# A source-block pass on one core: q rows of 3 of 13 cell groups gathered by GpSimd instead of multiplied by TensorE

## The chip, the cores and the metric

One core of a Trainium2 chip runs the whole program. The metric is the time of one execution in microseconds; three runs of the kernel before took 3949.36 to 3950.79 us, median 3950.47. Differences of the change are small, so all times are given to 0.1 us.

## The reference

The program is two graph layers with a layer norm behind each. The change touches the first:

```python
row, col = edge_index                       # 200,000 edges, 6,250 nodes, sorted by col
ef = concat([x[row], x[col], edge_attr])    # 128 + 128 + 2 features
h = ef @ W1 + b1                            # = p[row] + q[col] + attr @ W1[256:]
h = relu((h - mean(h)) * rsqrt(var(h) + 1e-5) * gamma + beta)
msgs = h @ W2 + b2
out = segment_sum(msgs, row) / (count(row) + 1) + x
```

p and q are x times the two halves of W1, so an edge's hidden row is a sum of a row of p (by its source), a row of q (by its target) and a product of its two attributes. The second layer is three graph convolutions, which the change leaves alone.

## The kernel before, in words

The 6,250 nodes make 49 blocks of 128. The bucket pass (`drive` with `step`, about 100 to 1250 us) sorts the edges into cells: a cell (source block b, target block c) has 128 slots, and for every slot it writes the place of its source and of its target within the block, and the attributes, to DRAM (`lrow_dram`, `arow_dram`). In each of its steps ScalarE copies TensorE's result `pbk` to `lo_all` (L997) and to `cells` (L998), and TensorE's next product (L873) waits for the latter.

The source-block pass (phase two, 1303 to 2655 us) goes over the 49 source blocks b, and in a block over 13 groups of cells: 12 of four cells, the last of one. Four quarters of T (`QUARTERS`: groups 0-2, 3-5, 6-8, 9-12) hold the places of source (T[k][:, 0]) and target (T[k][:, 1]) of every slot, spread over the partitions by a broadcast DMA from SP (L1237); VectorE turns them into 0/1 matrices by one compare (L1427).

For a group g each engine does, in its own order written out by hand:
- TensorE, `hidden(g)`: the attributes' product into a PSUM bank (L1291), then for each cell three matmuls with p (L1296) and three with q (L1298), since p and q are held as three bf16 parts each. Then `sums(g - 3)`: each cell's z times `hotf`, the 0/1 matrix of slots to sources, into `pSum` (L1312).
- ScalarE: Relu of the bank, rounded to bf16 (L1347, semaphore z_hi); then `middle(g - 1)`, which rounds what is left over (L1340, z_mid).
- VectorE: `left(g)` (L1439), bank minus z_hi, to `res` (z_res); then `low(g - 1)` (L1444), `res` minus z_mid, the third part of z (z_low). After g = 3 comes `quarter(b, 3)`, after g = 4 `take_sum` (L1450, L1452), after g = 6, 9, 12 `quarter(b + 1, 0..2)`; a quarter is the compare of T (L1427) and that of `hotf` (L1434).
- GpSimd does nothing in this pass; in the bucket pass it adds an identity to one 128x128 tile a step (L779).

There are four full PSUM banks (and `z`, `res` buffers), group g using number g % 4, and one small one for group 12. `sums(g)` waits for z_low of g, and TensorE may take the bank of g - 4 once `left` has read it.

Of the kernel before, what the change touches and what calls it, by code (L numbers as in the profile page):

```python
# [19 lines left out]
F32 = mybir.dt.float32  # L20
# [9 lines left out]
ROWS = B * P  # L30
# [21 lines left out]
QCELLS = (12, 12, 12, 13)  # L52
STRIP = 512
# [474 lines left out]
def build(nc, t, out):  # L528
# [7 lines left out]
    with outer:  # L536
        def mk(ctx):
# [36 lines left out]
             chunk_used y_taken yt_ready tail_done ln_ask ln_root out_ready out_sent dv3 root_b x_in bias_done g_taken""".split()})  # L574
        t_in = [fit_sem(f"t_in{u}") for u in range(4)]
        attr_rows = [fit_sem(f"attr_rows{u}") for u in range(2)]
        a_in = [fit_sem(f"a_in{u}") for u in range(7)]
# [32 lines left out]
        with early:  # L610
            sb, _ = mk(early)
            q3 = sb("q3", [P, B, 3, D], BF16)
            q3_flat = q3[:].rearrange("p b m d -> p (b m d)")
            prod_raw = sb("prod_raw", [P, 2 * 4 * TPB * B], BF16)
# [16 lines left out]
            with one:  # L631
# [17 lines left out]
                class Carve:  # L649
# [3 lines left out]
                    def take(self, n):  # L653
# [31 lines left out]
                q3st = [sb(f"q3st{u}", [P, 4, 3, D], BF16) for u in range(2)] + [q3_flat[:, NF * COLS:NF * COLS + 12 * D].rearrange("p (b m d) -> p b m d", b=4, m=3)]  # L685
                q3st.append(in_x1f.take(6 * D).bitcast(BF16).rearrange("p (b m d) -> p b m d", b=4, m=3))
                q3_sent = q3_out + [S["pf_in"]]
# [12 lines left out]
                          (pid1[:], t["pid1"])]  # L700
# [7 lines left out]
                def sp_1(sp):  # L708
# [64 lines left out]
                def pool_1(pool):  # L773
# [7 lines left out]
                    drive(pool, step)  # L781

# [121 lines left out]
                def act_1(act):  # L904
# [52 lines left out]
                    def step(s, m, par, bkt, h_, a_, y_, st_):  # L957
# [33 lines left out]
                        if bkt:  # L991
# [5 lines left out]
                            nc.scalar.activation(lo_all[:, :, s:s + 1] if isinstance(s, int) else lo_all[:, :, bass.ds(s, 1)], got[:, 0:1, :].rearrange("p f b -> p b f"), ACT.Copy)  # L997
                            nc.scalar.activation(cells[par][:, 0:8, 0:B], got, ACT.Copy).then_inc(S["cells_ready"], 1)  # L998
                    drive(act, step)
# [185 lines left out]
            with two:  # L1185
# [17 lines left out]
                st = ps("st", [P, 512])  # L1203

# [20 lines left out]
                def sp_2(sp):  # L1225
# [8 lines left out]
                    def quarter(b, k):  # L1234
                        c0 = 4 * QUARTERS[k][0]
                        rows = lrow_dram[b:b + 1] if isinstance(b, int) else lrow_dram[bass.ds(b, 1)]
                        sp.dma_start(T[k], rows[:, :, c0:c0 + QCELLS[k], :].rearrange("a f c s -> a f (c s)").to_broadcast([P, 2, QCELLS[k] * P])).then_inc(t_in[k], 16)  # L1237
# [19 lines left out]

                def pe_2(pe):
# [17 lines left out]
                    pe.wait_ge(S["q3_in"], 16)  # L1276
# [594 lines left out]
```

## Time and profile before

| | us |
|---|---|
| median of 3 runs | 3950.47 |
| profiled execution | 3951.36 |
| its span, first to last instruction | 3949.5 |
| TensorE (PE) busy over the span | 3769.3 |
| VectorE (DVE) busy | 2573.1 |
| ScalarE (ACT) busy | 1395.4 |
| GpSimd (POOL) busy | 85.1 |

Busy times are sums of durations of single instructions, seen as one where they overlap. Matmuls are pipelined: each of 128 columns is shown as 220 ns long, while a new one starts every 55 ns. So the pace of TensorE is read from the chain of waits, whose pieces don't overlap. L numbers are lines of the kernel before.

### The profile page before, as it was taken

To read this page: it belongs to the slowest core of one execution; us is meant where nothing else is said; L and a number is where in the kernel's file an instruction comes from. 1 tells how busy PE (TensorE), PEld (TensorE's weight loads), DVE (VectorE), ACT (ScalarE), POOL (GpSimd) and SP (SyncE) were. 2 spreads that over 40 slices of the span, in tenths; PEclk is the share of its full clock that TensorE was granted. 3 is DMA by queue.
4 is the path that set the end of the run, shared out by engine and by line. 5 is a ranking of instruction groups with operands and counts; after the bars stand their busy time and mean duration, and the time that the engine had idled before them with its cause. 6 is when DMAs were issued, how large, how long until landed. Compare 5 with 4: busy or idle time off the path is not lost.

```text
span 3949.5 us, 104146 instructions
## 1 busy us (share of the span) xinstructions
PE 3769.3 (95%) x42510; PEld 2695.9 (68%) x42510; DVE 2573.1 (65%) x3609; ACT 1395.4 (35%) x3527; POOL 85.1 (2%) x53
## 2 busy tenths in 40 slices
PE   4699999999998799999999999997999999999999
PEld 3488888888887688887888888884444444454444
DVE  7999999999993688888888888875111111111222
ACT  5355555545543355554555455545000000000000
POOL 0000000000000000000000000000000000000000
PEclk9899999999998899999999999999999999999999
DMA  7123223232233733333333333334666566656664
GB/s 238 51 83 99 84 87 93 84 96 88 81 98 140 122 126 129 133 122 125 124 132 131 124 126 129 126 114 144 196 196 197 188 199 196 196 189 207 211 204 139
DMA packets 397700, 547.34 MB, mean 139 GB/s; under 512 B 175743, under 2 KB 335240, under 8 KB 390440
## 3 DMA queue, kind: packets, MB, share of 16 engines
q1 hardware_dynamic: 390856, 537.51, 42.9%
q10 hardware_dynamic: 6624, 6.42, 0.5%
q8 instruction: 196, 3.21, 0.3%
q14 instruction: 24, 0.20, 0.0%
HBM read 434.34 MB, written 109.53 MB: 138 GB/s over the span
## 4 chain that ended last, share of the span: by engine, by line
PE 91%; DVE 4%; SPq 2%; ACT 1%; issue 1%; DMA 1%; ACTq 0%; DVEq 0%
PE py L1579 29%; PE pY L835 10%; PE ph L1298 10%; PE ph L1296 10%; PE pSum L1312 10%; PE pbk L896 8%; PE pA L822 3%; PE ph L1291 3%; PE pX L827 2%; PE pS L826 1%; PE pbk L873 1%; PE ptr L881 1%; DVE prod_raw L1120 1%; PE pg L1567 1%; SPq L1245 1%
## 5 line engine op out<-in xcount | busy, mean ns | idle before, releaser
L1579 PE MATMUL py<-ring_raw,p 128*128 128x512 bf16 (+1 forms) x3822 | 783.4, 367 | 18.0 <-DVE dummy L1739 16.1
L1298 PE MATMUL ph<-q,prod_raw 128*128 128x128 bf16 x7056 | 781.7, 220 | 0.8 <-issue 0.8
L1296 PE MATMUL ph<-p,prod_raw 128*128 (+1 forms) x7056 | 780.9, 220 | 0.0
L1579 PEld LDWEIGHTS py<-ring_raw,p 128*128 128x128 bf16 x3822 | 362.2, 98 | 430.9 <-DVE dummy L1739 16.5
L1296 PEld LDWEIGHTS ph<-p,prod_raw 128*128 128x128 bf16 x7056 | 518.6, 98 | 110.9 <-issue 2.7
L1347 ACT ACTIVATE x<-ph 128x512 bf16<-128x512 f32 x588 | 351.2, 597 | 668.0 <-PE ph L1298 664.7
L1439 DVE SCALAR_TENSOR_TENSOR ring_raw<-ph,x 128x512 f32<-128x512 f32 x588 | 404.3, 688 | 182.0 <-ACT x L1347 170.8
L1312 PE MATMUL pSum<-x,ring_raw 128*128 128x384 bf16 x2401 | 499.6, 327 | 8.9 <-DVE x L1444 8.9
L835 PE MATMUL pY<-p,ring_raw 128*128 128x128 bf16 x7203 | 501.0, 219 | 0.2 <-issue 0.2
L1298 PEld LDWEIGHTS ph<-q,prod_raw 128*128 128x128 bf16 x7056 | 495.8, 98 | 0.0
L1755 DVE TENSOR_TENSOR yt<-py,dinv_row 128x512 f32<-128x512 f32 (+1 forms) x39 | 25.8, 661 | 697.1 <-PE py L1579 697.1
L955 ACT ACTIVATE ring_raw<-pA 128x512 bf16<-128x512 f32 (+1 forms) x637 | 357.9, 571 | 250.5 <-PE pA L822 247.7
L1444 DVE TENSOR_TENSOR x<-ring_raw,x 128x512 bf16<-128x512 f32 (+1 forms) x637 | 414.4, 651 | 0.1
L835 PEld LDWEIGHTS pY<-p,ring_raw 128*128 128x128 bf16 x7203 | 409.3, 97 | 0.4 <-issue 0.4
L1579 PE MATMUL py<-ring_raw,g 128*128 128x512 bf16 (+1 forms) x1911 | 392.8, 368 | 1.9 <-DVE dummy L1767 1.9
L1632 ACT ACTIVATE hT<-yt,cb 128x512 f32<-128x512 f32 (+1 forms) x39 | 27.2, 697 | 1036.9 <-DVE yt L1755 1036.9
L1340 ACT ACTIVATE x<-ring_raw 128x512 bf16<-128x512 f32 (+1 forms) x637 | 381.4, 599 | 11.9 <-DVE ring_raw L1439 10.4
L1120 DVE TENSOR_TENSOR prod_raw<-q 128x1666 bf16<-128x1666 bf16 x392 | 375.5, 1020 | 12.7 <-PE pbk L896 11.6
L1093 DVE TENSOR_TENSOR ring_raw<-iota_lo,x 128x3584 bf16<-128x3584 bf16 x196 | 355.1, 1872 | 12.7 <-PE pX L827 12.7
L896 PE MATMUL pbk<-prod_raw,q 128*128 128x392 bf16 x1666 | 321.7, 350 | 28.1 <-DVE q L1093 28.1
L1579 PEld LDWEIGHTS py<-ring_raw,g 128*128 128x128 bf16 x1911 | 181.4, 98 | 209.0 <-issue 2.2
L896 PEld LDWEIGHTS pbk<-prod_raw,q 128*128 128x128 bf16 x1666 | 161.5, 98 | 170.2 <-issue 35.6
(322 smaller groups left out, 3906.0 us busy)
## 6 DMA issues: line engine op xcount, KB each, us to landing
ring_raw<-at_dram SPq DMA_DIRECT2D x252, 896.0 KB, 4.8
prod_raw<-lrow_dram SPq DMA_DIRECT2D x147, 768.0 KB, 4.2
at_dram<-ring_raw SPq DMA_DIRECT2D x49, 1568.0 KB, 5.6
prod_raw<-lrow_dram SPq DMA_DIRECT2D x49, 832.0 KB, 4.3
arow_dram<-x SPq DMA_DIRECT2D x147, 73.5 KB
x<-arow_dram SPq DMA_DIRECT2D x147, 54.0 KB
q<-q_dram SPq DMA_DIRECT2D x1, 4704.0 KB, 25.6
ring_raw<-at_dram SPq DMA_DIRECT2D x21, 224.0 KB, 2.5
```

The costliest lines, as they stand in the source:

```text
L835: last = nc.tensor.matmul(pY[:, 0:D], abuf[1 - par][:, b, :], p3[:, b, m3, :], start=b == m3 == 0, stop=b == B - 1 and m3 == 2)
L896: last = nc.tensor.matmul(pbk[:, 0:8 * B], orank[:, i // 2, :, i % 2], prod[:, :, i // 2, :, i % 2], start=i == 0, stop=i == TPB - 1)
L955: nc.scalar.activation(abuf[u][:, 4 * g:4 * g + w, :], pA[(g + u) % 2][:, 0:w * P].rearrange("p (b d) -> p b d", d=P), ACT.Copy).then_inc( ...
L1093: return V.tensor_tensor(to, iota_lo[:].unsqueeze(1).to_broadcast(dims), of.unsqueeze(2).to_broadcast(dims), ALU.is_equal)
L1120: return V.tensor_tensor(prod[:, f, :, :, :], hot_p, rec[u][:, 2 + f, :].rearrange("p (g u) -> p g u", u=2).unsqueeze(2).to_broadcast(dims ...
L1296: nc.tensor.matmul(bank[:, k * P:(k + 1) * P], T[q][:, 0, at:at + P], p_b[:, :, m3, :].rearrange("p a d -> p (a d)"), start=False, stop=False)
L1298: last = nc.tensor.matmul(bank[:, k * P:(k + 1) * P], T[q][:, 1, at:at + P], q3[:, c, m3, :], start=False, stop=m3 == 2 and k == w - 1)
L1312: last = nc.tensor.matmul(pSum[u][:, 0:3 * D], hotf[q][:, at // 2, :, at % 2], zb[which(g)][:, k, :, :].rearrange("p m d -> p (m d)"), sta ...
L1340: nc.scalar.activation(zb[which(g)][:, 0:w, 1, :], res[which(g)][:, 0:w, :], ACT.Copy).then_inc(S["z_mid"], 1)
L1439: V.scalar_tensor_tensor(out=res[u][:, 0:w, :], in0=banks[u][:, 0:w * P].rearrange("p (c d) -> p c d", d=D), scalar=0.0, in1=zb[u][:, 0:w, ...
L1444: V.tensor_tensor(zb[u][:, 0:w, 2, :], res[u][:, 0:w, :], zb[u][:, 0:w, 1, :], ALU.subtract).then_inc(S["z_low"], 1)
L1579: last = nc.tensor.matmul(py[par][:, 0:w], g3[c % 2][:, 7 * i + m, k, :], ring[i][:, 0:w // P, m, :], start=i == m == k == 0, stop=i == m ...
```

## The change

`TAKEN = (2, 5, 8)`: in these three groups of each block TensorE does not multiply by q. GpSimd instead gathers, for each of the 4 x 128 slots, the f32 row of q from DRAM (four indirect DMAs of 128 rows of 512 B a group, twelve a block, 588 in all), one block ahead. VectorE adds the rows to the bank (`add_q`), ScalarE and VectorE go on from `res`, and GpSimd, not VectorE, forms the third part of z of these groups (`third`). The quarters 0 to 2 of T lose the target half of four cells. In the bucket pass ScalarE also keeps the targets' places (`tgt_all`), of which GpSimd makes row numbers at its end; one more constant is loaded, and q3 is loaded in four pieces.

```diff
+TAKEN = (2, 5, 8)
+THOTS = tuple(sum(4 if g < 12 else 1 for g in range(lo, hi) if g not in TAKEN) for lo, hi in QUARTERS)
 # sp_1
-                            sp.dma_start(q3[:], q3_dram).then_inc(S["q3_in"], 16)
+                            for lo, hi in zip([0] + [4 * g + 4 for g in TAKEN], [4 * g for g in TAKEN] + [B]):
+                                sp.dma_start(q3[:, lo:hi, :, :], q3_dram[:, lo:hi, :, :]).then_inc(S["q3_in"], 16)
 # pool_1, after its steps
+                    for i, g in enumerate(TAKEN):
+                        base = row_base[:, 4 * g:4 * g + 4].unsqueeze(1).to_broadcast([P, B, 4])
+                        nc.gpsimd.tensor_tensor(taken_rows[i], tgt_all[:, 4 * g:4 * g + 4, :].rearrange("p c b -> p b c"), base, ALU.add).then_inc(S["a_final"], 1)
 # act_1, in each step
                             nc.scalar.activation(lo_all[...], got[:, 0:1, :]..., ACT.Copy)
+                            nc.scalar.activation(tgt_all[...], got[:, 1:2, :], ACT.Copy)
                             nc.scalar.activation(cells[par][:, 0:8, 0:B], got, ACT.Copy).then_inc(S["cells_ready"], 1)
 # sp_2, quarter: two DMAs where the target half is shorter
+                            for f, n in enumerate((QCELLS[k], THOTS[k])):
+                                sp.dma_start(T[k][:, f, 0:n * P], rows[:, f, c0:c0 + n, :].rearrange("a c s -> a (c s)").to_broadcast([P, n * P])).then_inc(t_in[k], 16)
 # pool_2
+                    def gather(b, i):
+                        row = taken_rows[i][:, b:b + 1, :] if isinstance(b, int) else taken_rows[i][:, bass.ds(b, 1), :]
+                        nc.gpsimd.tensor_copy(chosen[i][:].unsqueeze(1), row).then_inc(S["rows_chosen"], 1)
+                        put(pool, S["rows_chosen"], b * len(TAKEN) + (i + 1))
+                        for k in range(4):
+                            nc.gpsimd.indirect_dma_start(q_rows[i][:, k, :], None, pq_rows, bass.IndirectOffsetOnAxis(ap=chosen[i][:, k:k + 1], axis=0)).then_inc(q_rows_in[i], 16)
+                    def third(b, i):
+                        u = which(TAKEN[i])
+                        put(pool, S["z_mid"], b * 13 + (TAKEN[i] + 1))
+                        nc.gpsimd.tensor_tensor(zb[u][:, :, 2, :], res[u], zb[u][:, :, 1, :], ALU.subtract).then_inc(S["z_low_taken"], 1)
+                    for i in range(len(TAKEN)):
+                        gather(0, i)
+                    with pool.Fori(1, B) as b:
+                        for i in range(len(TAKEN)):
+                            third(b - 1, i)
+                            put(pool, S["q_added"], b * len(TAKEN) + (i + 1 - len(TAKEN)))
+                            gather(b, i)
 # pe_2, hidden and sums
-                            for m3 in range(3):
+                            for m3 in range(0 if g in TAKEN else 3):
                                 last = nc.tensor.matmul(bank[...], T[q][:, 1, at:at + P], q3[:, c, m3, :], ...)
+                        if g in TAKEN:
+                            pe.wait_ge(S["z_low_taken"], b * len(TAKEN) + (TAKEN.index(g) + 1))
 # act_2, one_block
+                            if g in TAKEN:
+                                middle(b, g - 1)
+                                act.wait_ge(S["q_added"], b * len(TAKEN) + (TAKEN.index(g) + 1))
+                                hidden = res[which(g)][:, 0:w, :]
 # dve_2
+                    def add_q(b, g):
+                        u, i = which(g), TAKEN.index(g)
+                        dve.wait_ge(S["mm_done"], b * 13 + (g + 1))
+                        dve.wait_ge(q_rows_in[i], b * 64 + 64)
+                        V.tensor_tensor(res[u], banks[u].rearrange("p (c d) -> p c d", d=D), q_rows[i], ALU.add).then_inc(S["q_added"], 1)
                         for g in range(13):
+                            if g in TAKEN:
+                                add_q(b, g)
+                                low(b, g - 1)
                             left(b, g)
```

`left(b, g)` of a taken group reads `res` instead of the bank, and `low(b, g)` of one returns at once.

## Rows read from the trace of the kernel before

**Rows 1.** Busy us of PE, PEld, DVE, ACT, POOL; clock, DMA share, GB/s.

```profile
1400.00:2640.00 1240.00, 1233.91 (x16151) 1019.89 (x16150) 1066.86 (x1631) 630.80 (x1180) 0.00 (x0) 1.00 0.37 127
```

**Rows 2.** Chain of waits, 1990 to 2050 us: start us, length us, engine, tile, line.

```profile
1990.56 0.22 PE ph L1291
1990.94 0.17 PE ph L1298 x3
...
1992.11 0.66 PE pSum L1312 x4
...
1994.32 0.66 PE pSum L1312 x4
...
1999.80 0.66 PE pSum L1312 x4
...
2026.91 0.66 PE pSum L1312 x4
```

**Rows 3.** Waits of VectorE, 1400 to 2640 us: total, times, longest.

```profile
DVE ring_raw L1439 <- ACT x L1347: 154.2, 185, 4.4
DVE ring_raw L1452 <- DVE s_raw L1450: 8.1, 44, 0.2
```

**Rows 4.** Timeline of VectorE in one block: start, length; [idle before].

```profile
2001.42 1.01 DVE L1427 TENSOR_SCALAR prod_raw<-prod_raw,pid 128x3072 bf16<-128x3072 bf16 x1
2002.35 0.95 DVE L1434 TENSOR_TENSOR ring_raw<-iota_lo,x 128x1536 bf16<-128x1536 bf16 x1
2003.22 0.68 DVE L1439 SCALAR_TENSOR_TENSOR ring_raw<-ph,x 128x512 f32<-128x512 f32 x1
...
2008.90 0.69 DVE L1439 SCALAR_TENSOR_TENSOR ring_raw<-ph,x 128x512 f32<-128x512 f32 x1 [0.43 <-ACT x L1347]
2009.51 0.68 DVE L1444 TENSOR_TENSOR x<-ring_raw,x 128x512 bf16<-128x512 f32 x1
2010.11 1.08 DVE L1427 TENSOR_SCALAR prod_raw<-prod_raw,pid 128x3328 bf16<-128x3328 bf16 x1
2011.10 1.08 DVE L1434 TENSOR_TENSOR ring_raw<-iota_lo,x 128x1792 bf16<-128x1792 bf16 x1
...
2013.31 0.55 DVE L1450 TENSOR_REDUCE s_raw<-pSum 128x128 f32<-128x384 f32 x1
...
2014.31 0.69 DVE L1439 SCALAR_TENSOR_TENSOR ring_raw<-ph,x 128x512 f32<-128x512 f32 x1
```

**Rows 5.** Timeline of ScalarE and TensorE where a step of the bucket pass begins.

```profile
707.66 0.40 ACT L997 ACTIVATE x<-pbk 128x49 f32 x1 [5.89 <-PE pbk L896]
707.77 0.62 ACT L998 ACTIVATE x<-pbk 128x392 bf16<-128x392 f32 x1
...
708.53 1.05 PE L873 MATMUL pbk<-q,upper 128*128 128x49 bf16 x34 [0.17 <-ACT x L998]
```

**Rows 6.** Timeline of ScalarE in the same block.

```profile
2006.55 0.60 ACT L1347 ACTIVATE x<-ph 128x512 bf16<-128x512 f32 x1 [1.10 <-PE ph L1298]
2007.05 0.62 ACT L1340 ACTIVATE x<-ring_raw 128x512 bf16<-128x512 f32 x1
```

**Rows 7.** Timeline of GpSimd in the bucket pass.

```profile
249.64 2.19 POOL L779 TENSOR_TENSOR ring_raw<-ring_raw,identb 128x128 bf16 x1 [20.33 <-ACT ring_raw L955]
...
678.99 1.64 POOL L779 TENSOR_TENSOR ring_raw<-ring_raw,identb 128x128 bf16 x1 [20.88 <-ACT ring_raw L955]
701.47 1.83 POOL L779 TENSOR_TENSOR ring_raw<-ring_raw,identb 128x128 bf16 x1 [20.84 <-ACT ring_raw L955]
...
1248.82 0.42 POOL L779 TENSOR_TENSOR ring_raw<-ring_raw,identb 128x128 bf16<-128x128 bf16 x1 [26.84 <-ACT ring_raw L955]
```

**Rows 8.** Timeline of VectorE: the compares beside which L779 falls, or not.

```profile
157.14 7.02 DVE L1093 TENSOR_TENSOR ring_raw<-iota_lo,x 128x3584 bf16<-128x3584 bf16 x4
...
179.90 7.25 DVE L1093 TENSOR_TENSOR ring_raw<-iota_lo,x 128x3584 bf16<-128x3584 bf16 x4
```

**Rows 9.** Timeline of SP's queue: issues of a constant and of a tile.

```profile
4.28 0.53 SPq L714 DMA_DIRECT2D iota_c<-in_iota_c  x1
...
1249.32 0.34 SPq L764 DMA_DIRECT2D at_dram<-ring_raw  x1
```

**Rows 10.** DMA issues, 1400 to 2640 us: count, size, median us to landing.

```profile
prod_raw<-lrow_dram SPq DMA_DIRECT2D x135, 768.0 KB, 4.2
```

**Rows 11.** Waits, 1303 to 1400 us, the start of the pass.

```profile
PE ph L1291 <- DVE prod_raw L1427: 11.9, 1, 11.9
```

More of the change, by code:

```diff
@@ L1203, in build @@
                 st = ps("st", [P, 512])
+                chosen = [sb(f"chosen{i}", [P, 4], I32) for i in range(len(TAKEN))]
+                pq_rows = pq_dram.rearrange("a r d -> (a r) d")
+                T_IN = tuple(16 + 16 * (QCELLS[k] != THOTS[k]) for k in range(4))
                 def which(g):
@@ L1256, in pool_2 @@
                     pool.wait_ge(S["rows_set"], 1)
+                    def gather(b, i):
[15 more added lines that the diff above has]
+                            gather(b, i)
+                    for i in range(len(TAKEN)):
+                        third(B - 1, i)
                 def pe_2(pe):
@@ L1295, in hidden @@
                             for m3 in range(3):
-                                nc.tensor.matmul(bank[:, k * P:(k + 1) * P], T[q][:, 0, at:at + P], p_b[:, :, m3, :].rearrange("p a d -> p (a d)"), start=False, stop=False)
-                            for m3 in range(3):
+                                last = nc.tensor.matmul(bank[:, k * P:(k + 1) * P], T[q][:, 0, at:at + P], p_b[:, :, m3, :].rearrange("p a d -> p (a d)"), start=False, stop=g in TAKEN and m3 == 2 and k == w - 1)
+                            for m3 in range(0 if g in TAKEN else 3):
                                 last = nc.tensor.matmul(bank[:, k * P:(k + 1) * P], T[q][:, 1, at:at + P], q3[:, c, m3, :], start=False, stop=m3 == 2 and k == w - 1)
@@ L1344, in one_block @@
                             w = len(group(g))
-                            act.wait_ge(S["mm_done"], b * 13 + (g + 1))
+                            if g in TAKEN:
+                                middle(b, g - 1)
+                                act.wait_ge(S["q_added"], b * len(TAKEN) + (TAKEN.index(g) + 1))
+                                hidden = res[which(g)][:, 0:w, :]
+                            else:
+                                act.wait_ge(S["mm_done"], b * 13 + (g + 1))
+                                hidden = banks[which(g)][:, 0:w * P].rearrange("p (c d) -> p c d", d=D)
                             bank_free(act, S["sum_done"], b, g)
-                            nc.scalar.activation(zb[which(g)][:, 0:w, 0, :], banks[which(g)][:, 0:w * P].rearrange("p (c d) -> p c d", d=D), ACT.Relu).then_inc(S["z_hi"], 1)
-                            if g >= 1:
+                            nc.scalar.activation(zb[which(g)][:, 0:w, 0, :], hidden, ACT.Relu).then_inc(S["z_hi"], 1)
+                            if g in TAKEN:
+                                pass
+                            elif g >= 1:
                                 middle(b, g - 1)
```

44 lines of the change are left out of this document (33 added, 11 removed).

## The prediction

> **What bounds the kernel now.** I read the totals by stretch first. In the source-block pass (1303 to 2655 us of the span) TensorE is busy 1233.91 of 1240 us at a granted clock of 1.00, the level of 2.4 GHz, and VectorE 1066.86 of 1240; GpSimd does nothing [rows 1]. Then the chain of waits: in this stretch it holds TensorE's pieces alone. One block repeats every 2026.91 - 1999.80 = 27.11 us, one group of four cells every 1994.32 - 1992.11 = 2.21 us, and a step of three q matmuls takes 0.17 us in it [rows 2]. Then the waits: VectorE waits for ScalarE 154.2 us and for itself 8.1 us of the 1240 [rows 3], 13.1%, so it works 27.11 x 0.869 = 23.56 us a block. So TensorE bounds the pass with VectorE 3.5 us a block behind it. The timeline gives VectorE's real pitch, start to start, which is below the durations since instructions overlap: `left` 2009.51 - 2008.90 = 0.61, `low` 0.60, the compare of T 0.93 for 3072 columns and 0.99 for 3328, the `hotf` compare 0.87, `take_sum` 1.00 [rows 4]. In the bucket pass before it (100 to 1250 us) TensorE is again on the chain, and waits 0.17 us for ScalarE's copy of the cells [rows 5].
>
> **TensorE's part.** Removed are 12 matmuls in each of 3 groups. A group is 0.22 (L1291) + 24 matmuls + 0.66 (sums) = 2.21, so a matmul takes 1.33/24 = 0.0555 us, 12 take 0.67 (four times the 0.17 of [rows 2]) and 36 take 2.0. A block would be 27.11 - 2.0 = 25.1 us; over 49 blocks -98 us is all there is to win.
>
> **VectorE's work.** Three `low` leave it (-3 x 0.60) and three `add_q` come: a 128x512 addition of PSUM and SBUF, not in the trace as such; its neighbours `left` (PSUM and SBUF) and `low` (both SBUF) take 0.60 to 0.61 of pitch, so +3 x 0.60, with no wider bounds than their durations, 0.65 to 0.69 [rows 4]. These cancel. Three compares of T lose 512 columns each; 256 columns more cost 0.06 us [rows 4], so -3 x 0.13 = -0.4. `left` of a taken group reads SBUF for PSUM: the same pitch. That leaves 23.2 us. In a taken group the order is `add_q`, `low` of the group before, then `left`, which waits until ScalarE (0.60 after `add_q` is done [rows 6]) has made z_hi: `low` hides 0.60 of some 0.74, so 0.14 idle, 3 x 0.14 = 0.4. Together 23.6, still below 25.1. ScalarE has room, it works 1.1 of 2.2 us a group [rows 6].
>
> **GpSimd beside VectorE** is what decides, and the bucket pass shows it. GpSimd's 128x128 addition takes 0.42 us with VectorE idle beside it, and 1.83 or 1.64 beside VectorE's compares with two SBUF inputs [rows 7]: it waits for the compare that runs to end. VectorE pays as well: four such compares take 7.02 us when no GpSimd operation falls into them (that at 157.14) and 7.25 when one does (that at 179.90) [rows 8], 0.23 us for 128 columns. `third` has 512 columns: between 0.42 and 4 x 0.42 = 1.68 us alone, I take 1.3, since most of 0.42 must grow with the columns if 0.23 of it is a hold of VectorE; and it takes from VectorE 4 x 0.23 = 0.92 us at most when the two meet, 0 when not. They do meet: z_mid of groups 2, 5 and 8 is finished by ScalarE 0.5 us after its Relu of groups 3, 6 and 9, which is when VectorE ends `left` of those groups, and exactly behind these stand its `quarter` compares. The T compare goes first (0.9 us of delay for `third`), `third` enters at its end, and the `hotf` compare waits. So I take 3 x 0.95 = 2.85 us with the change-over (ends 0 and 3.9, the latter if `third` shuts VectorE out for its whole 1.3).
>
> The page "SBUF — State Buffer" of the Trainium skill (Who interferes with whom) says that a VectorE instruction with two SBUF inputs contends with a GpSimd one that reads SBUF, as an exclusive lock on a shared port, and that a compare in a two-port mode shuts out descriptor writing as well. The trace agrees for the first (1.83 against 0.42); by the full lock the loss would be 3 x 1.3 = 3.9 us a block instead of 2.85. No run shows the second.
>
> Three copies of 128x4 indices on GpSimd and its reading of 12 index columns also touch VectorE: 0 to 15 x 0.23 = 3.4 us; I take 0.25, as they are 4 and 1 columns against 128. VectorE then has 23.6 + 2.85 + 0.25 = 26.7 us a block: it, not TensorE, sets the period, 0.41 us below 27.11.
>
> **The gathers.** A gather of 128 rows of 512 B is in no row. From below: SP issues a plain DMA in 0.34 us; from above: a hindered GpSimd operation, 2.19 us [rows 7, 9]. The middle is 1.27; I take 1.2 us of GpSimd's time for each. Landing is hidden: rows are asked for a block ahead and a DMA lands in some 4.2 us [rows 10]; 49 x 12 x 64 KB is 38.5 MB over 1.35 ms, 28 GB/s on 127, with the DMA engines 0.37 busy [rows 1]. Between `third` of two taken groups stand one index copy and four gathers: 1.3 + 0.3 + 4 x 1.2 = 6.4 us. VectorE's own work from group 6 to 9 is 1.66 + 6 x 0.60 + 0.14 + 0.95 = 6.35 us, from 3 to 6 it is 7.7 (quarter 2.0, take_sum 1.0). So 1.2 us just fits and nothing is added. From 8 to 2 of the next block GpSimd has over 12 us. TensorE's own slack for `third`: sums(g) start 0.66 + 1.55 + 0.66 + 0.89 = 3.76 us after hidden(g+1), and z_low could be there 0.28 + 0.49 + 0.62 + 1.3 = 2.7 after it: 1.1 us to spare, which the T compare's 0.9 uses up.
>
> The page "DMA: Bandwidth & Descriptors" (Specifications) gives about 1 us for the first byte on GpSimd's path; if that were all emission, the gathers would take 12 us a block and fit.
>
> **The bucket pass.** ScalarE has one more copy of 128x49 in front of the cells' copy. L997 and L998 start 0.11 us apart though L997 lasts 0.40 [rows 5], and TensorE waits for this result (0.17 us in one step, starts right at its end in the next): +49 x 0.11 = 5.4 us, up to 49 x 0.40 = 19.6. A gain is excluded, nothing leaves there. GpSimd's three index sums come when only TensorE's last products run (1250 to 1259) and are hidden. SP gets one more constant (0.53 us [rows 9]), three more DMAs for q3 and three more for T per block, each some 0.45 us; in the pass they lie in SP's waits, at its start they stand before block 1, whose T already lands late: +1 us together, 0 to 12 (TensorE lost 11.9 us once there [rows 11]; gathers now share these engines).
>
> **Sum.** Profiled time 3951.4 (span 3949.5); -48 periods x 0.41 = -19.7; +5.4 +1.0: 3938.1. The profile lies 0.9 us above the median of the runs, so **3937 us**.
>
> **The rivals.**
> - TensorE sets the pace (18%). If GpSimd's reads cost VectorE little, it has 23.6 to 24.5 us under TensorE's 25.1 and a period is 25.3 with some waits for `third`: -48 x 1.8 = -87, time 3870. For it: 0.23 us per 128 columns may be mostly fixed. Against it: the compares and `third` meet by construction.
> - GpSimd's gathers are too long (28%), the slower side. From 1.2 us a gather on, `third` of group 8 comes late by 4 x the excess, from 1.5 that of group 5 too; TensorE's sums stand still, less some 1.1 us of spare per block. At 1.7 us: (8.4 - 6.35) + (8.4 - 7.7) - 1.1 = 1.65 a block, period 28.35, +60 + 6.5: 4016. It is slower than before from about 1.55 us on (4 x 0.35 = 1.4, of which 1.1 is spare). For it: every GpSimd operation beside a busy VectorE takes four times its 0.42 [rows 7]. Against: the bound from SP.
> - The latency of a taken group eats the gain (12%), so that the change doesn't do what it says: matmul, add, Relu, `left`, copy, `third` is one chain over three engines with 1.1 us to spare; if each of three groups stops TensorE for 0.67 us, the period stays 27.1 and only the bucket pass's cost is left: 3957.
>
> **Numbers.** The forecast has 42%, its own range is 3915 to 3960. A change within 0.2% (8 us) can't be told from none. Faster: 30 of the forecast's 42 and 18, 48%. Same: 11 and 5 of the last rival's, 16%. Slower: 1, 28 and 7, 36%. The range, with a tenth on either side left out at most: 3866 (TensorE's pace) to 4040 (gathers of 1.75 us).
>
> **What would show it.** The period of L1312's pieces: 26.7, or 25.3, or above 27.1. VectorE's idle time in 1400 to 2640: near none for the forecast, over 10% for the gathers. The compare at L1434 after groups 3, 6, 9 longer or later by about 0.9; `third` near 1.3 us alone and over 2 from its issue; GpSimd's interval between gathers near 1.2. TensorE's wait before L1312 put down to GpSimd would speak for the second or third rival; L873's wait in the bucket pass should grow from 0.17 to 0.28. The forecast is wrong if VectorE has idle time and TensorE waits for GpSimd.

## The result

| | before | after |
|---|---|---|
| time, median, us | 3950.5 (4 runs) | 4126.0 (4 runs, 4124.4 to 4129.7) |
| ratio to before | | 1.0441, interval 1.0428 to 1.0455 |
| span of the profiled execution, us | 3949.5 | 4125.3 |
| period of a block, median of 48, us | 27.11 | 30.49 |

The kernel is 4.4% slower, by 175.4 us. The period is taken from the starts of the Relu of group 12, once a block. By the mean period, 30.83 against 27.33, 48 x 3.50 = 168 of the 175 us lie in the source-block pass.

The totals of the pass; the columns are those of [rows 1]. Of 1240 us TensorE is now busy 1074.29 in place of 1233.91, at a mean granted clock of 0.95 in place of 1.00:

```profile
1400.00:2640.00 1240.00, 1074.29 (x12637) 853.99 (x12815) 1014.58 (x1440) 579.30 (x1041) 746.36 (x722) 0.95 0.42 125
```

The waits of the same stretch (total, times, longest):

```profile
POOL x L1293 <- ACT x L1389: 274.2, 40, 13.6
ACT x L1402 <- PE ph L1344: 190.9, 153, 9.0
ACT x L1402 <- remote: 158.2, 53, 4.4
DVE ring_raw L1504 <- ACT x L1402: 132.8, 132, 7.1
...
DVE ring_raw L1504 <- issue: 74.4, 37, 2.8
...
PE pSum L1361 <- POOL x L1293: 101.3, 47, 2.5
```

No engine is full. TensorE's sums (L1361) wait for GpSimd 101.3 us, though the gathers do not cause all of this: e1_no_gather below, which has none, still has 57.8 us of it. ScalarE's Relu (L1402) waits 158.2 us for "remote", a release that the profile can put down to no engine. VectorE waits 215 us where [rows 3] had 162. Two things stand behind this, and one block shows both.

**The third part comes late.** Timeline of GpSimd:

```profile
2007.41 1.81 POOL L1293 TENSOR_TENSOR x<-ring_raw,x 128x512 bf16<-128x512 f32 x1 [6.62 <-ACT x L1389]
2009.17 1.04 POOL L1285 CAST chosen<-q 128x4 int32 x1
2011.00 1.22 POOL L1288 DMA_INDIRECT q<-pq_dram,chosen  x1 [0.79 <-POOL chosen L1285]
2012.52 0.95 POOL L1288 DMA_INDIRECT q<-pq_dram,chosen  x1 [0.30 <-issue]
2013.78 1.41 POOL L1288 DMA_INDIRECT q<-pq_dram,chosen  x1 [0.30 <-issue]
2015.49 1.16 POOL L1288 DMA_INDIRECT q<-pq_dram,chosen  x1 [0.30 <-issue]
2016.66 1.17 POOL L1293 TENSOR_TENSOR x<-ring_raw,x 128x512 bf16<-128x512 f32 x1
```

The third part of group 5 (2016.66) waits for nothing but the gather ahead of it. From one third part to the next 9.25 us pass. TensorE waits for it, and runs at half clock afterwards (timeline of TensorE, where the last number is the wait before a row; then the stretch behind it by the columns of [rows 1]):

```profile
2013.71 0.82 PE L1361 MATMUL pSum<-x,ring_raw 128*128 128x384 bf16 x4
2014.59 0.83 PE L1342 MATMUL ph<-p,prod_raw 128*128 x12
2017.88 1.46 PE L1361 MATMUL pSum<-x,ring_raw 128*128 128x384 bf16 x4 [2.47 <-POOL x L1293]
```

```profile
2017.88:2021.30 3.42, 3.42 (x24) 2.45 (x25) 2.89 (x5) 1.46 (x3) 2.04 (x4) 0.53 0.59 211
```

The same four sums take 1.46 us in place of 0.82: after 2.47 us without work TensorE was granted 0.53, the level of 1.2 GHz. In the clock's record 37 such stretches, 130 us, lie in the pass from 1350 us on; before there were 2, with 10 us. 35 of the 37 begin within 0.5 us of the end of a pause of TensorE of 2.3 to 2.5 us.

**TensorE's counts come late.** TensorE ends the first group of a block at about 1999.5 (the same engine's next sums start at 1999.38). The count that tells of it rises at 2001.71, and ScalarE, whose Relu waits for nothing else, starts at 2001.81, 2.3 us later. First TensorE's timeline, then ScalarE's:

```profile
1999.22 0.33 PE L1344 MATMUL ph<-q,prod_raw 128*128 128x128 bf16 x3
1999.38 0.82 PE L1361 MATMUL pSum<-x,ring_raw 128*128 128x384 bf16 x4
...
2001.59 0.33 PE L1342 MATMUL ph<-p,prod_raw 128*128 x3 [0.46 <-issue]
```

```profile
2001.81 0.60 ACT L1402 ACTIVATE x<-ph 128x512 bf16<-128x512 f32 x1 [3.44 <-remote]
2002.31 0.30 ACT L1389 ACTIVATE x<-ring_raw 128x128 bf16<-128x128 f32 x1
```

I compared each rise of a semaphore of TensorE in the trace with the ends of the matmuls that raise it. In the kernel before, all 1140 rises in 1400 to 2600 us come within 0.02 us of such an end. In the changed kernel 310 of 1003 come over 0.3 us behind the latest end before them. That is a lower bound where several rises come together: the ends at 2013.87 and 2015.42 have theirs at 2016.94 and 2017.13, 3.07 and 1.71 us late. None of the 2091 rises by the other engines does so. The profile models the ends of matmuls, so an end could itself be late; but these two ends lie 1.55 us apart and their rises 0.19 us, less than the 12 products between them take (0.67 us), so not all of the delay can be work that was done late: counts were held. They come out when a row of gathers is over: 215 of the 310 late rises follow the end of the fourth gather of a row within 1.2 us, a stretch that makes up 11% of the time, and in e12_spread_gathers below 221 of 236. TensorE itself stands still for short times then (0.46 <-issue above). Below, "late counts" are these.

### The profile page after: what moved, and what is told of

The parts are those of the page before. It is cut to its first block, busy times and chain, and to the rows that moved or that the text cites. A ratio compares the mean times of both kernels' runs of the same rounds, so it can differ in the third digit from the quotient of the medians.

```text
span 4125.3 us, 103479 instructions
## 1 busy us (share of the span) xinstructions
PE 3755.2 (91%) x40525; PEld 2638.3 (64%) x40746; DVE 2658.4 (64%) x3609; ACT 1425.1 (35%) x3576; POOL 993.2 (24%) x938
## 4 chain that ended last, share of the span: by engine, by line
PE 70%; DVE 10%; issue 7%; POOL 4%; ACT 3%; another core or an unknown queue 2%; SPq 2%; DMA 1%; POOLq 0%; ACTq 0%; DVEq 0%
PE py L1651 28%; PE pY L850 10%; PE pbk L911 8%; PE ph L1342 5%; PE pSum L1361 5%; PE pA L837 3%; PE ph L1344 3%; POOL q L1288 3%; DVE ring_raw L1504 2%; DVE prod_raw L1485 2%; ACT x L1402 2%; PE pX L842 1%; PE pS L841 1%; PE pbk L888 1%
## 5 line engine op out<-in xcount | busy, mean ns | idle before, releaser
L1342 PE MATMUL ph<-p,prod_raw 128*128 (+1 forms) x7056 | 736.2, 224 | 48.7 <-issue 24.1
L1288 POOL DMA_INDIRECT q<-pq_dram,chosen x588 | 621.2, 1057 | 257.9 <-issue 145.0
L1361 PE MATMUL pSum<-x,ring_raw 128*128 128x384 bf16 x2401 | 520.3, 337 | 147.0 <-POOL x L1293 121.1
L1344 PE MATMUL ph<-q,prod_raw 128*128 128x128 bf16 x5292 | 605.6, 224 | 9.4 <-issue 9.4
L1827 DVE TENSOR_TENSOR yt<-py,dinv_row 128x512 f32<-128x512 f32 (+1 forms) x39 | 25.8, 661 | 702.4 <-PE py L1651 702.3
L1504 DVE SCALAR_TENSOR_TENSOR ring_raw<-ph,x 128x512 f32<-128x512 f32 x441 | 302.2, 686 | 241.6 <-ACT x L1402 152.0
L1402 ACT ACTIVATE x<-ph 128x512 bf16<-128x512 f32 x441 | 262.6, 595 | 508.3 <-PE ph L1344 241.6
L1344 PEld LDWEIGHTS ph<-q,prod_raw 128*128 128x128 bf16 x5292 | 386.9, 101 | 12.1 <-issue 11.5
L1361 PEld LDWEIGHTS pSum<-x,ring_raw 128*128 128x128 bf16 x2401 | 210.1, 100 | 251.6 <-POOL x L1293 132.4
L788 POOL TENSOR_TENSOR ring_raw<-ring_raw,identb 128x128 bf16 (+1 forms) x49 | 80.3, 1638 | 1170.7 <-ACT ring_raw L970 1170.7
```

Of the source, the lines that this page charges most:

```text
L1288: nc.gpsimd.indirect_dma_start(q_rows[i][:, k, :], None, pq_rows, bass.IndirectOffsetOnAxis(ap=chosen[i][:, k:k + 1], axis=0)).then_inc(q_ ...
L1342: last = nc.tensor.matmul(bank[:, k * P:(k + 1) * P], T[q][:, 0, at:at + P], p_b[:, :, m3, :].rearrange("p a d -> p (a d)"), start=False, ...
L1344: last = nc.tensor.matmul(bank[:, k * P:(k + 1) * P], T[q][:, 1, at:at + P], q3[:, c, m3, :], start=False, stop=m3 == 2 and k == w - 1)
L1361: last = nc.tensor.matmul(pSum[u][:, 0:3 * D], hotf[q][:, at // 2, :, at % 2], zb[which(g)][:, k, :, :].rearrange("p m d -> p (m d)"), sta ...
L1504: V.scalar_tensor_tensor(out=res[u][:, 0:w, :], in0=hidden, scalar=0.0, in1=zb[u][:, 0:w, 0, :], op0=ALU.max, op1=ALU.subtract).then_inc(S ...
```

## Experiments

The theory at the start: the indirect gathers cost by the late counts, and by the third part that queues behind them. Its rivals: GpSimd's third part, which locks VectorE; the DMA traffic as such; VectorE's own order. Each run is an edit of the changed kernel, timed beside the kernel before (medians of 3949.4 to 3951.8 us in five groups of runs). P is the median period; "late" (rises of TensorE over 0.3 us late, 1400 to 2600 us) and "half clock" (in the pass, from 1350 us on) are worked out from the trace as above. e2_third_on_vector was timed twice, the others three to ten times.

| run | time | ratio, interval | P | late | half clock, us |
|---|---|---|---|---|---|
| after | 4126.0 | 1.0441, 1.0428 to 1.0455 | 30.49 | 310 | 130 |
| e1_no_gather | 3968.0 | 1.0055, 1.0032 to 1.0078 | 27.37 | 0 | 14 |
| e2_third_on_vector | 4018.4 | 1.0177, 1.0147 to 1.0206 | 28.78 | 478 | 10 |
| e3_vector_alone | 3947.9 | 0.9993, 0.9982 to 1.0004 | 26.85 | 0 | 14 |
| e4_plain_dma | 3968.8 | 1.0049, 1.0026 to 1.0071 | 27.37 | 0 | 14 |
| e10_half | 3963.5 | 1.0031, 1.0021 to 1.0041 | 27.37 | 0 | 14 |
| e11_gathers_between | 3982.4 | 1.0077, 1.0060 to 1.0094 | 27.73 | 0 | 14 |
| e5_rows_in_order | 4050.7 | 1.0243, 1.0225 to 1.0260 | 29.31 | 0 | 106 |
| e6_small_t | 4046.8 | 1.0241, 1.0224 to 1.0258 | 29.31 | 0 | 102 |
| e7b_vector_full_t | 3957.3 | 1.0018, 1.0009 to 1.0028 | 27.12 | 0 | 17 |
| e7_spread_vector | 3917.9 | 0.9916, 0.9899 to 0.9932 | 26.22 | 0 | 14 |
| e12_spread_gathers | 4089.6 | 1.0353, 1.0336 to 1.0370 | 29.87 | 236 | 17 |
| e14_full_t | 4131.3 | 1.0459, 1.0441 to 1.0476 | 30.56 | 305 | 102 |
| e17_paced | 3983.6 | 1.0082, 1.0064 to 1.0101 | 27.73 | 0 | 17 |
| e15_paced_spread | 3956.7 | 1.0017, 1.0008 to 1.0027 | 26.84 | 0 | 21 |
| e16_paced_vector | 3936.9 | 0.9963, 0.9949 to 0.9977 | 26.74 | 0 | 14 |
| e8_one_group | 3932.2 | 0.9954, 0.9936 to 0.9971 | 26.78 | 0 | 7 |
| e18_two_groups | 3895.6 | 0.9857, 0.9841 to 0.9874 | 26.01 | 0 | 10 |

### The parts of the change by themselves

**e1_no_gather**: `gather(b, i)` is left out from block 1 on. 

> Left out: 576 of the 588 gathers (those of block 0 stay), so blocks 1 to 48 add stale q rows; everything else is as in the changed kernel. Theory (the gathers cost it all: GpSimd's 1.25 us each hold up `third`, and beside them TensorE's semaphore counts arrive up to 3 us late): the period of a block falls from 30.4 us to 25.3 to 26.7, the time to 3870 to 3940, TensorE's clock stays at 1.00. Rival (GpSimd's `third` and VectorE block each other, the gathers matter little): the period stays above 28 us, the time above 4000.

**e2_third_on_vector**: VectorE forms all third parts, GpSimd only gathers.

```diff
-                            third(b - 1, i)
...
-                        if g in TAKEN:
-                            return
```

> `third` goes back to VectorE as `low`, the gathers stay; nothing is left out. Theory A (what costs is that `third` stands behind the gathers in GpSimd's queue): period 26 to 27 us, time 3900 to 3950. Theory B (what costs is that TensorE's semaphore counts arrive late beside the gathers, whoever makes the third part): the late counts stay, period 27.5 to 29.5, time 3975 to 4075.

**e3_vector_alone**: both edits, so GpSimd has no work in the loop. 

> Left out: 576 of the 588 gathers, as in e1, and `third` is VectorE's `low` again: GpSimd does nothing in the loop. If GpSimd's work is the whole loss, the pass runs at TensorE's pace of 25.1 us a block or VectorE's of 25.4: time 3860 to 3880. If the longer chain of a taken group (add, Relu, left, copy, low) costs by itself, it is above 3900.

**e4_plain_dma**: the same twelve DMAs by GpSimd, from fixed rows and not indirect.

```diff
-nc.gpsimd.indirect_dma_start(q_rows[i][:, k, :], None, pq_rows, bass.IndirectOffsetOnAxis(...))
+nc.gpsimd.dma_start(q_rows[i][:, k, :], pq_rows[ROWS + (4 * TAKEN[i] + k) * P:..., :])
```

> GpSimd issues plain DMAs of 128 fixed rows of 512 B in place of the indirect ones, so the q rows added are not the edges' own; number, bytes and order are the same. If it is any DMA that GpSimd issues that delays TensorE's semaphore counts, they are late by up to 3 us here too and the time is 4100 to 4130 (or less if its issue is shorter than 0.95 us). If it is the indirect form (reading indices, scattered rows), the counts are on time and the period falls below 28 us.

Against what was expected: e1 (3968.0) lies between the theory's 3940 and the rival's 4000, so neither the gathers nor the third part is the whole loss. TensorE waits for the third part there too:

```profile
PE pSum L1359 <- POOL x L1293: 57.8, 43, 1.4
```

In e2 theory B held, in e3 the case that the longer chain costs by itself (above 3900), and in e4 the indirect form (below 28 us, counts in time).

What they show: without gathers the third part on GpSimd costs 20 us (e1 less e3). Without any work of GpSimd the 98 us that TensorE saves bring 2 us (e3), which can't be told from none (interval 0.9982 to 1.0004). Plain DMAs cost nothing beside e1. Indirect ones cost 158 us with the third part on GpSimd (after less e1) and 70 without it (e2 less e3). The rows of GpSimd's DMA, of after and of e4:

```profile
L1288 POOL DMA_INDIRECT q<-pq_dram,chosen x588 | 621.2, 1057 | 257.9 <-issue 145.0 <-POOL chosen L1285 112.9
```

```profile
2004.83 2.14 POOL L1288 DMA_DIRECT2D q<-pq_dram  x4 [0.56 <-POOL chosen L1285]
```

An indirect one lasts 1.06 us and the next starts after another 0.30; four plain ones together last 2.14.

### How many, and where they stand

**e10_half**: two gathers a group from block 1 on.

```diff
-                        for k in range(4):
+                        for k in range(4 if isinstance(b, int) else 2):
```

> Two of the four gathers of each taken group are left out from block 1 on (the other rows stay those of block 0), so GpSimd gathers for 7.5 us of each block in place of 15. Theory (TensorE's counts come late while indirect gathers run, and each late count is paid once): the cost over the kernel with plain row DMAs (3969) goes with the time in which gathers run, so about half of 157 us is left: 4045 us (4025 to 4065), period about 28.9 us, late counts on about half as many of TensorE's groups. Rival (what costs is that the third part of group 5 stands behind four gathers, and the clock that falls after it): with two gathers less ahead of it, it is never late, nearly all goes, 3975 to 3995, period 27.4 to 27.8, and no stretch at half clock.

**e11_gathers_between**: three gathers behind the third part of group 2, three behind that of 5, six behind that of 8.

```diff
-                            gather(b, i)
+                            for n, ks in (((0, (0, 1, 2)),), ((0, (3,)), (1, (0, 1))), ((1, (2, 3)), (2, (0, 1, 2, 3))))[i]:
+                                rows(b, n, ks)
```

> The whole computation; only GpSimd's order is changed: three gathers behind the third part of group 2, three behind that of group 5, six behind that of group 8, from where ten groups pass before the next one. So at most three gathers stand ahead of a third part that TensorE wants soon. Theory (late counts cost 70 us by themselves, the queue on GpSimd and the clock that falls with it the rest, 87 us): 4045 to 4075 us, period 29.0 to 29.4, the clock at half in fewer than 10 stretches. Rival (all is late counts): 4110 to 4130, unchanged. Rival (all is the queue): 3970 to 3990.

**e5_rows_in_order**: the index table holds the partition's number.

```diff
-nc.gpsimd.tensor_tensor(taken_rows[i], tgt_all[...], base, ALU.add)
+nc.gpsimd.tensor_tensor(taken_rows[i], pid1[:, 0:1].unsqueeze(2).to_broadcast([P, B, 4]), base, ALU.add)
```

> The indirect DMAs stay as they are, but the table of rows holds row p for partition p (other values: the q rows of the taken groups are wrong, the work is the same). Theory (the indirect form itself does it, wherever the rows lie): unchanged, 4115 to 4135 us, gather 1.05 us, period 30.4. Rival (128 scattered rows of 512 bytes take the memory or the queues longer than rows in one piece): 3970 to 4050, and the counts come in time.

**e6_small_t**: `quarter(b + 1, k)` on SP becomes a DMA of 16 partitions. 

> The broadcasts of T (about 3 MB per block, by SyncE) are left out from block 1 on, with a DMA of 16 partitions in their place, so T keeps the rows of block 0; gathers and all else stay. Theory (late counts come from the indirect form alone): the period falls by at most 0.5 us, 4095 to 4130 us, and counts are still up to 3 us late. Rival (gathers and broadcasts crowd the same DMA engines, and the counts wait there): 3970 to 4010 us, no count over 0.3 us late.

My theory lost in the first two, and its rival held: half the gathers cost nothing, and all twelve in another order cost 14 us over e1, without a late count (the ranges put the rival at 3975 and above for e10, which came out lower still). In e5 the time came out just above the rival's upper end (4050), in e6 between theory and rival. The late counts were gone in both, as the rivals said, but about 80 us stayed over e1, which neither side had. What stayed is the other mechanism by itself. GpSimd's timeline in e6, where the third part again starts right behind the fourth gather:

```profile
2027.73 1.15 POOL L1293 DMA_INDIRECT q<-pq_dram,chosen  x1 [0.30 <-issue]
2028.91 1.17 POOL L1298 TENSOR_TENSOR x<-ring_raw,x 128x512 bf16<-128x512 f32 x1
```

and its wait and totals of 1400 to 2600 us: 122.1 us of TensorE for the third part, clock 0.96, while the DMA engines carry 37 GB/s in place of 125:

```profile
PE pSum L1366 <- POOL x L1298: 122.1, 62, 2.4
```

```profile
1400.00:2600.00 1200.00, 1072.77 (x13012) 859.97 (x13009) 1023.94 (x1464) 582.91 (x1058) 795.53 (x735) 0.96 0.15 37
```

So there are two mechanisms, each of some 70 us in this arrangement: a queue (third part behind four gathers, with the half clock it brings) and the late counts.

### Where the groups lie

**e7b_vector_full_t**: e3 with `THOTS = QCELLS`, T loaded and compared in full. 

> The kernel in which GpSimd has no work in the loop (3948), with groups 2, 5 and 8, but T loaded and compared in full; 576 of 588 gathers are left out. VectorE compares 3072 columns in place of 2560 three times in a block, 0.13 us each: 0.4 us. Theory (VectorE's order of work sets the period): period 27.1 to 27.3 us, 3960 to 3970. Rival (TensorE and latency set it): 26.85 us, 3948.

**e7_spread_vector**: e7b with `TAKEN = (1, 7, 10)`. 

> As the kernel in which GpSimd has no work in the loop (3948), but the taken groups are 1, 7 and 10 in place of 2, 5 and 8, and T is loaded and compared in full; 576 of 588 gathers are left out. Theory (groups 2, 5 and 8 are those before which VectorE does the compares of a quarter, about 2 us, so its longest stretches and TensorE's shortest groups fall together, and the gain on TensorE is lost in that): the period falls below that of the same kernel with groups 2, 5 and 8 and T in full by 0.5 to 1 us, to 26.0 to 26.7 us, 3905 to 3940. Rival (the chain add, Relu, left, middle, low through the banks costs the gain wherever the groups lie): no difference between the two beyond 0.1 us in the period.

**e12_spread_gathers**: the changed kernel with `TAKEN = (1, 5, 9)` and `THOTS = QCELLS`. 

> The whole computation with taken groups 1, 5 and 9 and T in full; GpSimd's order stays as in the changed kernel, but four groups (about 8.4 us) lie between two third parts, and copy with four gathers takes 6.3 us. Theory (what cost 87 to 144 us was that a third part stood behind four gathers with only three groups between): nearly all goes, no third part late, no stretch at half clock, period 27.4 to 28.0, 3965 to 3995 us, like the kernel with the gathers set between (3982). Rival (twelve indirect gathers in a row order of four cost by their counts wherever the groups lie): over 4040 us, with counts of TensorE over 1 us late.

**e14_full_t**: the changed kernel with `THOTS = QCELLS`. 

> The changed kernel with T loaded by one DMA per quarter and in full, as before the change (three DMAs less for each block, 1.2 MB more). The late counts of TensorE were gone when the rows lay in order, when T was not loaded, and when the gathers lay between. Theory (the gathers and the loads of T have to fall together, and it is their traffic): lateness stays, 4120 to 4150 us. Rival (the split of T's loads into two DMAs makes the counts late): no count over 0.3 us late, 4050 to 4075 us.

The place of the groups is worth 39 us without GpSimd (e7 against e7b; both periods came out in the theory's ranges and e7's time too, e7b's time 3 us below): VectorE's wait for the Relu falls from 59.0 us to 21.3 in 1200. First e7b, then e7:

```profile
DVE ring_raw L1494 <- ACT x L1392: 59.0, 90, 6.7
```

```profile
DVE ring_raw L1494 <- ACT x L1392: 21.3, 52, 5.4
```

In e12 the rival won: the third parts waited for ScalarE and not behind gathers, the clock was 0.99, and it still took 4089.6 us. TensorE's waits for the third part, 46.7 us, are shorter than in e1. Here the late counts stand alone. ScalarE's wait for them, TensorE's own stalls, and the totals, 1400 to 2600 us:

```profile
ACT x L1402 <- remote: 169.8, 94, 2.4
...
PEld ph L1344 <- issue: 36.7, 61, 1.3
PEld ph L1342 <- issue: 35.1, 67, 1.3
```

```profile
1400.00:2600.00 1200.00, 1036.61 (x12568) 820.09 (x12748) 1001.86 (x1434) 561.73 (x1035) 721.84 (x717) 0.99 0.45 142
```

e14 came out in the theory's range with 305 late counts, which rules out the split of T's loads as their cause.

### The order that takes both out

**e17_paced**: the changed kernel, GpSimd's loop rewritten so that it waits for each group and issues one gather behind it (two behind group 12). The edit sets the earliest time of each gather; it does not keep them apart where GpSimd is behind.

```diff
-                        for i in range(len(TAKEN)):
-                            third(b - 1, i)
-                            put(pool, S["q_added"], b * len(TAKEN) + (i + 1 - len(TAKEN)))
-                            gather(b, i)
+                        for g in range(13):
+                            put(pool, S["z_mid"], b * 13 + (g + 1 - 13))
+                            if g in TAKEN:
+                                third(b - 1, TAKEN.index(g))
+                            for i, k in SLOTS.get(g, ()):
+                                if k == 0:
+                                    put(pool, S["q_added"], b * len(TAKEN) + (i + 1 - len(TAKEN)))
+                                    choose(b, i)
+                                row_of(i, k)
```

> The whole computation, groups 2, 5 and 8 as in the changed kernel; GpSimd waits for each group of cells and issues one gather behind it (two behind group 12), so no two of the four stand in a row. Theory (counts come late when four scattered gathers go out in a row beside T's loads, and the third part is late behind them): both go, no count over 0.3 us late, no stretch at half clock, period 27.4 to 27.9, 3968 to 3990 us. Rival (each indirect gather has a price of its own, wherever it stands): over 4020 us.

**e15_paced_spread**: e17 with `TAKEN = (1, 5, 9)`, T in full, one gather behind each of groups 1 to 12. 

> The whole computation, groups 1, 5 and 9, T in full, one gather behind each of the groups 1 to 12, third part on GpSimd. Theory: the two causes out, and VectorE's order eased as with groups 1, 7 and 10 (26.2 us without GpSimd), plus 0.5 to 0.9 us for the third parts on GpSimd: period 26.7 to 27.2, 3935 to 3965 us. Rival (late counts stay with groups so spread, as in the spread kernel with four in a row, 4090): over 4020.

**e16_paced_vector**: e15 without `third`, as in e2. 

> As the last one, but VectorE forms the third part of every group and GpSimd only gathers: the whole computation. Theory: period 26.2 to 26.6 us, 3912 to 3940 us, faster than the kernel before. Rival (the gathers still cost 0.4 us of each block or more): 3940 to 3965 us.

**e8_one_group**: the changed kernel with `TAKEN = (8,)`. 

> The whole computation with one taken group, 8, and its four gathers in a row: a third of the gathers. Theory (the price goes with the rows of four): TensorE saves 0.67 us of each block, and one row of four gives back 0.65 us by late counts and 0.3 us by the third part on GpSimd, period 27.3 to 27.6, 3960 to 3975 us, late counts on about a third as many groups. Rival (late counts need the gathers of several groups together): none late, period 26.9 to 27.2, 3940 to 3957 us.

**e18_two_groups**: e16 with `TAKEN = (2, 8)` and the shorter T. 

> The whole computation with two taken groups, 2 and 8, one gather behind each of the groups 2 to 5 and 8 to 11, third part on VectorE. Theory (one group is bounded by TensorE, 1186 us busy of 1200 in its pass; a second takes 0.67 us off each block, and six or seven groups between the taken ones let VectorE catch up): period 26.1 to 26.4 us, 3895 to 3918 us. Rival (VectorE's order or its locks bind from two groups on, as with three): 26.7 us, 3930 to 3945.

e17 and e15 came out in the theory's ranges, e16 by its time (its period, 26.74, is 0.14 above). In e8 the rival held, and by more than it said (3932 below its 3940): four gathers in a row of one group make no late count, so the price does not go with their number. e18 is 1.4% faster than before, in the theory's range by its time (its period, 26.01, is 0.09 below).

The new order takes the late counts out, but not by the means that I expected. e17's expectation says that "no two of the four stand in a row"; in the traces they do. What GpSimd waits for before a gather has often come already, and the gathers follow each other. In e15, 1400 to 2600 us, there are 123 rows of four gathers with only 0.30 us between them. In e12, which has the same taken groups and the same loads of T, there are 114. GpSimd's timeline in e15, with the third part right behind the fourth gather:

```profile
2018.12 0.92 POOL L1286 CAST chosen<-q 128x4 int32 x1
2019.80 1.23 POOL L1290 DMA_INDIRECT q<-pq_dram,chosen  x1 [0.77 <-POOL chosen L1286]
2021.34 0.94 POOL L1290 DMA_INDIRECT q<-pq_dram,chosen  x1 [0.30 <-issue]
2022.58 0.94 POOL L1290 DMA_INDIRECT q<-pq_dram,chosen  x1 [0.30 <-issue]
2023.83 1.29 POOL L1290 DMA_INDIRECT q<-pq_dram,chosen  x1 [0.30 <-issue]
2025.14 1.17 POOL L1302 TENSOR_TENSOR x<-ring_raw,x 128x512 bf16<-128x512 f32 x1
```

Of e15's 1088 counts none is late; e12 has 236 late ones and takes 133 us more. So rows of four scattered gathers beside T's loads are not enough to hold the counts. The two kernels differ in GpSimd's waits between the gathers and, through them, in when a row falls within the block; which of the two matters no run shows. Nor are waits between the gathers needed: e11, which has none, only another order, took as long as e17 (3982.4 and 3983.6 us).

The totals of e17, e8 and e18, 1400 to 2600 us, show the bound move from VectorE to TensorE:

```profile
1400.00:2600.00 1200.00, 1090.50 (x13628) 872.54 (x13626) 1118.74 (x1534) 613.66 (x1108) 870.83 (x767) 0.99 0.47 137
```

```profile
1400.00:2600.00 1200.00, 1185.96 (x15296) 969.34 (x15294) 1075.38 (x1601) 625.47 (x1155) 304.48 (x264) 1.00 0.41 134
```

```profile
1400.00:2600.00 1200.00, 1189.41 (x15178) 966.37 (x15176) 1113.87 (x1735) 654.41 (x1188) 418.59 (x450) 1.00 0.45 140
```

## Why the prediction was wrong

The 175 us as differences of runs (medians, the runs of before beside them agree within 2.4 us): TensorE's saving as VectorE lets it through -2 (e3); third part on GpSimd +20 (e1 less e3); twelve gathers in an order that holds nothing up long +16 (e17 less e1); third part behind four gathers and the clock after it +67 (e5 less e17); late counts +75 (after less e5). Sum 176. The split of the last two rests on e5 taking away the late counts alone; e6, by another way, gives 63 and 79. The price of late counts is not a constant: e12 lies 133 us above e15, and e2, with 478 of them, 70 above e3.

Step by step:

- **TensorE's part**, -2.0 us a block: right in size. With one group taken TensorE is 99% busy at 26.78 us, where it was to be 27.11 - 0.67 = 26.4; with two (e18) the period is 26.01, where it was to be 25.8.
- **VectorE sets the pace with nothing idle**: the bound was right, "23.6 + 2.85 + 0.25 = 26.7" was not. In e3, where VectorE keeps the third parts, its work is by my terms 23.2 + 1.8 = 25.0; its instructions, each by its start-to-start time where nothing holds it up, add up to 24.6 of the 26.85 us of one block (1999.41 to 2026.26). So the work was counted well; the 0.4 too much are waits that the profile's list leaves out as too short, and that I therefore took for work. The other 2.2 us are idle, where I had 0.4, most of them waits for ScalarE, the longest 0.94 us. All quarters' compares follow the very groups that are short on TensorE. Taken groups set elsewhere give 0.9 of it back (e7). In e1, which has neither gathers nor late counts, the period is 27.37 for the forecast's 26.7: 32 us over 48 blocks.
- **Three locks of VectorE, 2.85 us**: right in mechanism and in size. The compare of `hotf` shows a lock by itself. In e1 a third part on GpSimd falls beside it in three groups of a block, and from its start to the next instruction's 2004.49 - 2002.65 = 1.84 us pass; in e3, where GpSimd is idle, 2013.33 - 2012.46 = 0.87. That is 0.97 us a lock, against my 0.95, and 2.9 a block. VectorE's timeline in e1, then in e3:

```profile
2002.65 1.92 DVE L1490 TENSOR_TENSOR ring_raw<-iota_lo,x 128x1536 bf16<-128x1536 bf16 x1
2004.49 0.68 DVE L1502 SCALAR_TENSOR_TENSOR ring_raw<-ph,x 128x512 f32<-128x512 f32 x1
```

```profile
2012.46 0.95 DVE L1482 TENSOR_TENSOR ring_raw<-iota_lo,x 128x1536 bf16<-128x1536 bf16 x1
2013.33 0.68 DVE L1494 SCALAR_TENSOR_TENSOR ring_raw<-ph,x 128x512 f32<-128x512 f32 x1
```

  The Trainium skill's page "SBUF — State Buffer" (Who interferes with whom) has this as an exclusive lock of the shared port. The trace agrees: 0.97 us more a compare, against a third part of 1.17 us alone.
- **A gather takes 1.2 us**: 1.25 from start to start where none is held up. Right.
- **"So 1.2 us just fits and nothing is added"**: this step failed. I had 6.4 us from one third part to the next, and 7.7 us of room for it from group 2 to group 5; it is 9.25 in the block above. The third part held up by VectorE takes 1.76 in place of 1.3, the copy of four indices 1.04 in place of 0.3, 0.79 us pass between this copy and the first gather, where I had nothing, and the four gathers take 5.66 in place of 4.8. I had written that the step has no room, and then priced every small term at its unhindered size. This is the rival "gathers too long" (28%) in its mechanism, by the queue around them and not by their length. Between groups 5 and 8, where I had seen the tightest place, 6.9 us pass (2016.66 to 2023.57). In e17's order 7.65 us lie between the third parts of groups 2 and 5, and 67 us are gone (e5 less e17).
- **TensorE's wait costs what it lasts**: it costs more. The clock fell in 37 stretches in 49 blocks. That was in no case of mine, and so the range ended at 4040: e5, which has the queue without late counts, lies at 4051 already.
- **What gathers cost beyond GpSimd's own time: no term in the sum**: they were put at nothing for TensorE's counts, without a reason, and this is the other step that failed. The late counts cost 75 us (after less e5). Nothing in the kernel before could show them, since none of its 1140 counts is late.
- **The latency of a taken group eats the gain** (12%): e3 looks like it (3948 and 26.85 against 3957 and 27.1), but e7 shows the order of VectorE's work behind most of it, not latency alone.
- **The bucket pass, +5.4**: it takes 2.9: the products of L873 run from 97.4 to 1183.8 us before and from 98.8 to 1188.1 now. The new copy does start 0.11 us behind the first and the cells' copy another 0.11 later, but TensorE waits 0.20 us for it where [rows 5] had 0.17, so by these spans about half of the 5.4 us is hidden; behind what, I did not measure. ScalarE's timeline, then TensorE's wait:

```profile
710.74 0.39 ACT L1012 ACTIVATE x<-pbk 128x49 f32 x1 [5.89 <-PE pbk L911]
710.85 0.32 ACT L1013 ACTIVATE q3st<-pbk 128x49 f32 x1
710.96 0.54 ACT L1014 ACTIVATE x<-pbk 128x392 bf16<-128x392 f32 x1
```

```profile
711.64 1.05 PE L888 MATMUL pbk<-q,upper 128*128 128x49 bf16 x34 [0.20 <-ACT x L1014]
```

- **Of the signs named for the trace**: VectorE idle 17% of the time (215 of 1240 us; over 10% was to speak for the gathers), TensorE waiting for GpSimd, and gathers near 1.2 us. The first two tell the case; the third, a gather's length, is the same in all runs, slow or not, so it decides nothing. TensorE's wait alone would mislead too, since e1 has more than half of it. Of the period, 30.49, the late counts make 1.2 us (less e5's 29.31), and no sign named them.

## What to carry to other kernels

Where an engine both computes something that others wait for and issues DMAs, count all that stands between two of its computations at its hindered length, the copy of indices and the pause behind it included; here 6.4 us by unhindered sizes became 9.25. If it does not fit, move DMAs to where more time lies between two computations: three gathers in place of four in the tightest place, and the rest later, was enough (e11). Look in the trace whether a new order does what it was made for, since e15's gathers still stood in rows. Do not shorten the same groups behind which another engine has its extra work. And take less of a good thing: two groups of four cells, with TensorE and VectorE both near full, gained 1.4% where three gained 0.4% at best in a kernel that does the whole work and cost 4.4% as first written.

## What the runs showed of the hardware

- Counts raised by TensorE reached other engines up to 3 us late, and TensorE stalled for up to 1.3 us, in four kernels in which GpSimd issued three rows of four scattered indirect gathers a block right behind the third parts or additions (310, 478, 236 and 305 late rises: after, e2, e12, e14). Most of the held counts came out within 1.2 us of the end of a row. There was none of it with plain DMAs (e4), two gathers in a row (e10), rows in order (e5), T's broadcasts left out (e6) or one taken group (e8), each an edit of the changed kernel, so several conditions must come together. There was none either in the orders of e11 and e15 to e18, although e15 has rows of four as e12 has. What the condition of time or order is, and what in the chip holds the counts back, is open, and no run measured it apart.
- An indirect gather of 128 rows of 512 bytes takes GpSimd 0.95 us alone and 1.06 to 1.20 us in the mean (after, e17), plus 0.30 us before the next; a plain DMA of the same size 0.54 (e4). The first gather starts 0.77 us after the copy that makes its indices.
- A third part of 1.17 us on GpSimd beside a VectorE compare with two SBUF inputs lengthens the compare by 0.97 us (e1 against e3).
- After pauses of TensorE of 2.3 to 2.5 us its clock was granted at 0.5 (1.2 GHz) for 3.4 us (after, 35 times).
